# One core, a fused attention and feed-forward kernel: the first tiles' statistics taken in twos, the first product in halves, and other work and loads in another order at the head

## The reference

```python
xn = (x - mean(x)) / sqrt(var(x) + 1e-5)
q, k, v = xn @ Wq + bq, xn @ Wk + bk, xn @ Wv + bv      # 32, 8, 8 heads of 16
scores = einsum('bsdh,bseh->bsde', q, repeat(k, 4)) / 4
s = einsum('bsde,bseh->bsdh', softmax(scores), repeat(v, 4)).reshape(1, 2048, 512)
nx = xn * rsqrt(mean(xn ** 2) + 1e-5) * ln_w
ffn = (silu(nx @ gate_w.T) * (nx @ up_w.T)) @ down_w.T   # inner width 1792
out = x + s * silu(ffn)
```

## Time and profile before

| | before |
|---|---|
| median of 3 runs | 474.47 us (474.45 to 474.83) |
| profiled execution | 474.35 us |
| its span, first to last instruction | 472.6 us |
| PE busy | 466.3 us, 99% of the span |
| DVE, ACT, POOL busy | 412.7, 244.2 and 123.1 us |
| DMA | 105.70 MB, 224 GB/s in the mean |

### The profile page before, as it was taken

One profiled execution on the slowest core, in us unless ns is written; L12 is line 12 of the kernel. 1 busy time (PEld: TensorE's weight loads), 2 busy tenths in 40 slices (PEclk: granted clock), 3 DMA queues, 4 the chain that ended last, 5 costly groups with the idle time before them and its releaser, 6 DMA issues.

```text
span 472.6 us, 6217 instructions
## 1 busy us (share of the span) xinstructions
PE 466.3 (99%) x2122; PEld 391.0 (83%) x2122; DVE 412.7 (87%) x561; ACT 244.2 (52%) x417; POOL 123.1 (26%) x106
## 2 busy tenths in 40 slices
PE   7999999999999999999999999999999999999997
PEld 7898888888888888888888888888888888888886
DVE  6889778987898898889989898999998888888994
ACT  4785656658588888654122545225225335358102
POOL 5740312126222122233443101000011111126920
PEclk9999999999999999999999999999999999999999
DMA  8605996579779996573474649546556655514772
GB/s 269 252 2 225 345 380 262 234 259 273 205 248 301 298 360 255 188 268 133 135 235 162 218 187 371 202 184 223 222 201 223 223 200 200 201 44 135 276 259 89
DMA packets 44623, 105.70 MB, mean 224 GB/s; under 512 B 20272, under 2 KB 21808, under 8 KB 41264
## 3 DMA queue, kind: packets, MB, share of 16 engines
q1 hardware_dynamic: 44592, 105.31, 63.3%
HBM read 69.90 MB, written 35.40 MB: 223 GB/s over the span
## 4 chain that ended last, share of the span: by engine, by line
PE 95%; DVE 2%; DMA 1%; ACT 1%; SPq 0%; POOL 0%; issue 0%
PE gu_ps L553 18%; PE gu_ps L555 18%; PE gu_ps L556 18%; PE y_ps L687 8%; PE y_ps L688 8%; PE y_ps L689 8%; PE gu_ps L688 3%; PE gu_ps L687 3%; PE gu_ps L689 3%; PE gu_ps L718 2%; PE gu_ps L715 2%; PE gu_ps L714 2%; DMA xz<-x 1%; DVE w_ops L1166 1%; PE y_ps L727 0%; DVE stats L1075 0%
## 5 line engine op out<-in xcount | busy, mean ns | idle before, releaser
L553 PE MATMUL gu_ps<-z_hi,w_ops 128*128 128x512 f32 x378 | 147.2, 390 | 0.1
L556 PE MATMUL gu_ps<-z_hi,w_ops 128*128 128x512 f32 x378 | 147.1, 389 | 0.0
L555 PE MATMUL gu_ps<-z_lo,w_ops 128*128 128x512 f32 x378 | 147.1, 389 | 0.0
L498 POOL TENSOR_TENSOR h_lo<-h,h_hi 128x512 fp32r<-128x512 f32 x28 | 37.4, 1335 | 226.8 <-ACT h_hi L916 226.6
L553 PEld LDWEIGHTS gu_ps<-z_hi,w_ops 128*128 128x128 f32 x378 | 71.0, 188 | 15.5 <-issue 0.4
L556 PEld LDWEIGHTS gu_ps<-z_hi,w_ops 128*128 128x128 f32 x378 | 70.9, 188 | 14.8
L555 PEld LDWEIGHTS gu_ps<-z_lo,w_ops 128*128 128x128 f32 x378 | 70.9, 188 | 14.5
L687 PE MATMUL y_ps<-wd_ops,h_hi 128*128 128x512 f32 x168 | 65.6, 390 | 0.0
L689 PE MATMUL y_ps<-wd_ops,h_lo 128*128 128x512 f32 x168 | 65.5, 390 | 0.0
L688 PE MATMUL y_ps<-wd_ops,h_hi 128*128 128x512 f32 x168 | 65.5, 390 | 0.0
L916 ACT ACTIVATE h_hi<-h 128x512 fp32r<-128x512 f32 x28 | 17.6, 630 | 58.9 <-DVE h L1208 58.9
(11 more groups left out here) (139 smaller groups left out, 753.0 us busy)
## 6 DMA issues: line engine op xcount, KB each, us to landing
w_kept<-w_ops SPq DMA_DIRECT2D x13, 1792.0 KB, 6.2
w_ops<-w_kept SPq DMA_DIRECT2D x13, 1792.0 KB, 7.6
wd_ops<-wd_kept SPq DMA_DIRECT2D x35, 512.0 KB, 4.0
raw<-gate_up SPq DMA_DIRECT2D x30, 256.0 KB, 3.9
wd_kept<-wd_ops SPq DMA_DIRECT2D x14, 512.0 KB, 7.8
xz<-x SPq DMA_DIRECT2D x16, 256.0 KB, 5.3
raw<-down SPq DMA_DIRECT2D x14, 256.0 KB, 8.5
w_ops<-wd_kept SPq DMA_DIRECT2D x7, 512.0 KB, 7.5
```

The source lines that it names most:

```text
L498: pool.tensor_tensor(lo, src, hi.bitcast(F32), ALU.subtract).then_inc(h_lo_done, 1)
L553: pe.matmul(acc, w_h, z_hi[:, zi, c, :], start=start and c == 0, stop=False, skip_group_check=True)
L555: pe.matmul(acc, w_h, z_lo[:, zi, c, :], start=False, stop=False, skip_group_check=True)
L556: end = pe.matmul(acc, w_l, z_hi[:, zi, c, :], start=False, stop=c == 1, skip_group_check=True)
```

## The change

All of it is at the head, in the first 23 us or so.

- **DVE**: statistics of tiles 0 and 1, then `bn_aggr` for each and one instruction for both variances; the same for tiles 2 and 3; then the four normalisations in a row. `x_variance(0)` comes behind `first_lo(0)`.
- **POOL**: one root for two tiles, twice; then the queries' sums; then the root and shift of tile 4; only then `rms_of(0, ...)`, which stood ahead of the sums; then the bias sums and tiles 5 to 7 as before.
- **PE**: `first_gate0` and `first_up0` become `first_products`. Gate's high by high product is made in halves of 256 columns, each behind its two tiles; gate's product with the low activations likewise, and up's high by high product stands between its halves. `qkv_product(0)` waits for the split weights in two steps, not at once.
- **ACT**: issues the load of `lnw` itself, first of all; `first_hi(1)` stands ahead of `z_raw` of tiles 0 and 1.
- **SP**: no `lnw`; up is loaded ahead of the query weights; x tiles 5 and 6 ahead of the biases.

```diff
             load_x(0, range(0, J))
-            sp.dma_start(lnw_sb[:], lnw).then_inc(lnw_in, 16)
             load_gate(0)
+            load_up(0)
             for a in (0, 2):
                 sp.dma_start(wq_raw[:, a:a + 2, :], wq.rearrange("(k p) n -> p k n", p=P)[:, a:a + 2, :])\
                   .then_inc(wq_in[a // 2], 16)
-            load_up(0)
             sp.dma_start(wqkv_raw[:, :, DG:2 * DG], wk.rearrange("(k p) n -> p k n", p=P)).then_inc(wkv_in, 16)
             sp.dma_start(wqkv_raw[:, :, 2 * DG:], wv.rearrange("(k p) n -> p k n", p=P)).then_inc(wkv_in, 16)
-            load_x(0, (J,))
+            load_x(0, range(J, JJ - 1))
             sp.dma_start(bq_raw, bq.partition_broadcast(P)).then_inc(bias_in, 16)
...
-            load_x(0, range(J + 1, JJ))
+            load_x(0, (JJ - 1,))
...
+            def scale_two(j):
+                pool.wait_ge(var_done, j + 2)
+                t = slice(j, j + 2)
+                pool.tensor_tensor(z_scale[:, t], z_var[:, t], minus_half[:, t], ALU.pow).then_inc(z_scale_done, 2)
+
             def scale_tile(j):
-                pool.wait_ge(var_done, j + 1 + (j >= J))
-                t = slice(j, j + 1)
+                pool.wait_ge(var_done, j + 2)
+                t, m = slice(j, j + 1), slice(j - J, j - J + 1)
...
-            for j in range(J):
-                scale_tile(j)
-            pool.wait_ge(var_done, J + 1)
-            rms_of(0, J, 1, 0)
+            scale_two(0)
+            scale_two(2)
             sum_queries(0)
             sum_queries(1)
             scale_tile(J)
+            pool.wait_ge(var_done, J + 1)
+            rms_of(0, J, 1, 0)
             pool.wait_ge(bias_in, 48)
...
+                pe.wait_ge(w_hi_a, 1)
+                for a, t in enumerate(halves):
+                    pe.wait_ge(z_hi_done, 2 * a + 2)
+                    for n, (wi, zi, c) in enumerate(gates):
+                        pe.matmul(gate[:, t], w_part(0, wi, c), z_hi[:, zi, c, t], start=a + n == 0, stop=False,
+                                  skip_group_check=True)
+                pe.wait_ge(w_lo_a, 1)
+                for wi, zi, c in gates:
+                    pe.matmul(gate, w_part(1, wi, c), z_hi[:, zi, c, :], start=False, stop=False, skip_group_check=True)
+                pe.wait_ge(z_lo_done, 2)
+                for wi, zi, c in gates:
+                    pe.matmul(gate[:, halves[0]], w_part(0, wi, c), z_lo[:, zi, c, halves[0]], start=False, stop=False,
+                              skip_group_check=True)
+                pe.wait_ge(w_hi_a, 2)
+                for n, (wi, zi, c) in enumerate(ups):
+                    pe.matmul(up, w_part(0, wi, c), z_hi[:, zi, c, :], start=n == 0, stop=False)
+                pe.wait_ge(z_lo_done, J)
...
-                pe.wait_ge(wqkv_hi_done, 2)
                 for k in range(K):
+                    if index == 0:
+                        pe.wait_ge(wqkv_hi_done, k // 2 + 1)
...
-                pe.wait_ge(wqkv_lo_done, 2)
                 for k in range(K):
+                    if index == 0:
+                        pe.wait_ge(wqkv_lo_done, k // 2 + 1)
...
+            act.dma_start(lnw_sb[:], lnw).then_inc(lnw_in, 16)
             load_silu()
...
+            first_hi(1)
             z_raw_tile(0)
             z_raw_tile(1)
-            first_hi(1)
...
+            for j in (0, 2):
+                stats_tile(j)
+                stats_tile(j + 1)
+                aggregate(j)
+                aggregate(j + 1)
+                two_variances(j)
             for j in range(J):
-                stats_tile(j)
-                if j:
-                    variance(j - 1)
-                if j > 1:
-                    normalise_tile(j - 2)
-            variance(J - 1)
-            normalise_tile(J - 2)
+                normalise_tile(j)
+            first_lo(0)
             x_variance(0)
-            normalise_tile(J - 1)
-            first_lo(0)
             for j in range(J):
                 z_lo_tile(j)
```

More of the change, by code:

```diff
@@ L575, in eight, with first_products, w_part @@
                 return end
-            def first_gate0():
-                acc = gu_ps[:, GATE_BANK, :]
-                chunks = [(wi, zi, c) for wi, zi in ((WA11, ZB11), (WA12, ZB21)) for c in range(2)]
-                pe.wait_ge(w_hi_a, 1)
-                pe.wait_ge(z_hi_done, J)
-                for n, (wi, zi, c) in enumerate(chunks):
-                    pe.matmul(acc, w_ops[:, 0, 0, wi, c * P:(c + 1) * P], z_hi[:, zi, c, :], start=n == 0, stop=False)
-                pe.wait_ge(w_lo_a, 1)
-                for wi, zi, c in chunks:
-                    pe.matmul(acc, w_ops[:, 0, 1, wi, c * P:(c + 1) * P], z_hi[:, zi, c, :], start=False, stop=False)
+            def first_products():
+                gate, up = gu_ps[:, GATE_BANK, :], gu_ps[:, UP_BANK, :]
+                gates = [(wi, zi, c) for wi, zi in ((WA11, ZB11), (WA12, ZB21)) for c in range(2)]
+                ups = [(wi, zi, c) for wi, zi in ((WA21, ZB11), (WA22, ZB21)) for c in range(2)]
+                halves = slice(0, TB // 2), slice(TB // 2, TB)
+                def w_part(s, wi, c):
+                    return w_ops[:, 0, s, wi, c * P:(c + 1) * P]
+                pe.wait_ge(w_hi_a, 1)
+                for a, t in enumerate(halves):
[3 more added lines that the diff above has]
+                                  skip_group_check=True)
+                pe.wait_ge(w_lo_a, 1)
+                for wi, zi, c in gates:
[7 more added lines that the diff above has]
+                    pe.matmul(up, w_part(0, wi, c), z_hi[:, zi, c, :], start=n == 0, stop=False)
@@ L587, in first_gate0 @@
                 pe.wait_ge(z_lo_done, J)
-                for n, (wi, zi, c) in enumerate(chunks):
-                    end = pe.matmul(acc, w_ops[:, 0, 0, wi, c * P:(c + 1) * P], z_lo[:, zi, c, :], start=False,
-                                    stop=n == 3)
+                for n, (wi, zi, c) in enumerate(gates):
+                    end = pe.matmul(gate[:, halves[1]], w_part(0, wi, c), z_lo[:, zi, c, halves[1]], start=False,
+                                    stop=n == 3, skip_group_check=True)
@@ L591, in first_gate0 @@
                 end.then_inc(m2_done, 1)
-            def first_up0():
-                acc = gu_ps[:, UP_BANK, :]
-                chunks = [(wi, zi, c) for wi, zi in ((WA21, ZB11), (WA22, ZB21)) for c in range(2)]
-                pe.wait_ge(w_hi_a, 2)
-                for n, (wi, zi, c) in enumerate(chunks):
-                    w_h = w_ops[:, 0, 0, wi, c * P:(c + 1) * P]
-                    pe.matmul(acc, w_h, z_hi[:, zi, c, :], start=n == 0, stop=False)
-                    pe.matmul(acc, w_h, z_lo[:, zi, c, :], start=False, stop=False)
+                for wi, zi, c in ups:
+                    pe.matmul(up, w_part(0, wi, c), z_lo[:, zi, c, :], start=False, stop=False)
@@ L601, in first_up0 @@
                 pe.wait_ge(w_lo_a, 2)
-                for n, (wi, zi, c) in enumerate(chunks):
-                    end = pe.matmul(acc, w_ops[:, 0, 1, wi, c * P:(c + 1) * P], z_hi[:, zi, c, :], start=False,
-                                    stop=n == 3)
+                for n, (wi, zi, c) in enumerate(ups):
+                    end = pe.matmul(up, w_part(1, wi, c), z_hi[:, zi, c, :], start=False, stop=n == 3)
                 end.then_inc(m4_done, 1)
@@ L1056, in _, with aggregate, two_variances, variance @@
         def _(dve):
-            def variance(j):
+            def aggregate(j):
                 dve.wait_ge(bn_done, j + 1)
                 dve.bn_aggr(mean_var[:, j, :], stats[:, j, :]).then_inc(stats_done, 1)
+            def two_variances(j):
+                dve.wait_ge(stats_done, j + 2)
+                dve.tensor_scalar(z_var[:, j:j + 2], mean_var[:, j:j + 2, 1], 1.0 + EPS, EPS * EPS,
+                                  ALU.mult, ALU.add).then_inc(var_done, 2)
+            def variance(j):
                 dve.wait_ge(stats_done, j + 1)
```

12 lines of the change are left out of this document (5 added, 7 removed).

## The result

| | before | after |
|---|---|---|
| median, taken in turns on one chip | 474.65 us (474.45 to 474.99, 4 runs) | 478.94 us (478.04 to 479.6, 4 runs) |
| profiled execution | 474.35 us | 479.6 us |
| its span | 472.6 us | 477.8 us |
| mean granted clock in it | 1.00 | 0.996 |

The ratio is 1.009, with an interval of 1.0072 to 1.0108: slower by 4.3 us, where 475.6 (+1.15) was forecast and 476.4 was the end of the range. The direction was right and the size was not.

A forecast was written before the change was run, and what follows sets the result against it. PE was taken to bound the kernel, its head paced by a tight line from POOL's tile 5 root to tile 2's product. -1.09 + 2.3 = +1.21, less 0.05 rounding, +1.15: 475.6 us, range 474.1 to 476.4.

The forecast's parts named there:

- -1.09 (sums sooner): POOL's queries' sums start at 10.35, not 11.44, so tile 4's statistics and shift come 1.09 us sooner.
- +2.3 (`rms_of` on the line): On POOL, `rms_of` now stands between tile 4's shift and the bias sums, delaying tile 5's root by 2.3 us.
- The clock: Rival D: PE's waits of 1.5 and 0.8 us drop it to 1.2 GHz, 2 us on top, 477.6; 4%.
- None of this reaches the tight line: Statistics in twos and `lnw` on ACT don't affect the line from POOL's tile 5 root to PE's tile 2 product.
- the bound of 0.48: Delay of an x tile from loading `lnw` on ACT's queue: between 0 and one issue step, 0.48 us.
- The product in halves at nothing: On PE, tile 0's first query product comes about 1.4 us sooner, then PE waits for tile 4: no gain.
- the shape of the wait: PE waits 1.5 us ahead of tile 5's transposes, then 0.8 us between those and tile 6's.
- The prediction's marks: Signs: POOL's 128x4 roots at 17.4 to 19.5, PE waiting over 2 us for `xz`, tile 2's product about 24.
- B: Rival: POOL's pair of `rms_of` roots is covered, POOL free some 0.9 us sooner: 474.4 to 475.3; 23%.
- C: Rival: transfers limit the head and all moves sooner; PE keeps 1.4 us from the first product: 473.1; 11%.
- B's own condition: `lo_qkv` on DVE comes later than POOL's tile 4 root, which alone takes 0.56 us, not 1.26.

The follow-up runs named there:

- a_lnw_sp: After, with the load of `lnw` back on SP behind x tiles 0 to 3: 476.9 us, ratio 1.0037 against before.
- a_sum_wait: After, with POOL's queries' sums waiting until DVE has made the low parts of gate's weights: 476.98 us, ratio 1.0042 against before.
- b_rms_late: Before, with one edit: `rms_of` moved behind tile 4's root and shift on POOL: 478.62 us, ratio 1.0075 against before.
- b_halves: Before, with only the PE and ACT part: first products in halves, finer waits, `first_hi(1)` ahead of `z_raw`: 474.83 us, ratio 0.9996.
- a_up_back: After, with up loaded behind the query weights again, `lnw` still on ACT: 477.66 us, ratio 1.0066 against before.
- a_lnw_fill: After, with `lnw` loaded by SP and 12 and 6 added transposes in PE's waits: 478.09 us, ratio 1.0068 against before.

## Why the prediction was wrong, by its own steps

- **The step that failed: "-1.09 (sums sooner)".** It took the sums' earlier start as a gain in full, and tile 4's statistics came 1.75 us later and not 1.09 sooner, an error of 2.84. Of this 2.42 is DVE held by the sums: 1.65 in `first_lo(0)` and 0.77 in the last normalisation. The other 0.42 is what the term was over-sized by without a collision, as far as one profile tells: in a_lnw_sp, where the sums missed `first_lo(0)`, tile 4's statistics came 0.66 sooner. The forecast of 475.6 with that error put right is 478.4, and after's two runs at full clock took 478.45 and 478.04. The prediction let the sums start at 10.35 and read `first_lo(0)` with the 1.05 that it took beside other work. It asked what the sums would be *rid* of (the overlap with `first_lo(1)`) and never what stood on DVE at the place that they move *to*. Its own rows had both: the query weights lay there from 9.6 on in before, and `first_lo(0)` ran from 9.56 to 10.61. With up ahead it let the weights land at 10.3; in after they let the sums start at 9.83, and these met the last normalisation and three of the four of `first_lo(0)`. The landing alone doesn't explain the error: from 10.35 on the sums would have met `first_lo(0)` too, which could start at 10.3 at the soonest (an estimate: 11.07 less 0.77).
- **The rule that was applied at one place only.** The prediction cited the Trainium skill, "SBUF — State Buffer", section "Who interferes with whom", and said that it speaks against a pure gain, but used it only for `first_lo(1)` and put no price on the place that the sums move to. By it a DVE instruction with two SBUF inputs and a GpSimd instruction that reads SBUF exclude each other. a_sum_wait and b_rms_late agree: four instructions of 0.34 us take 1.13 in all ahead of the sums and 2.77 to 3.66 beside them. Before doesn't, in one place: POOL's roots of 128x4 read SBUF too, and beside them the same four took no longer. There the measurement decides.
- **"+2.3 (`rms_of` on the line)" held**: 2.21 in the trace, 2.1 at tile 5's root when undone. So did its place, and the distance from there to PE.
- **"The clock", 4%, was too little.** The mechanism was named with its place; what was missing was how likely it is. It came in two of four runs and costs 1.56 us in the profiled one (said: 2). PE's waits were 1.34 and 0.56 us, less than the 1.5 and 0.8 that the rival assumed.
- **"None of this reaches the tight line", for the statistics in twos and `lnw`, held only in before's order.** Tile 3's statistics began 0.61 later in after's profile (7.14 against 6.53), more than the bound of 0.48, and the third and fourth normalisation wait for one root. Neither is dear by itself; together they moved `first_lo(0)` 0.8 us later, and the held normalisation as much again, to 11.07, under the sums. The root of 128x2 took 0.71 and 0.87 where 0.7 was taken.
- **The product in halves at nothing held** (b_halves, in before's order), and so did the shape of the wait. The prediction's marks were met late: roots of `rms_of` at 20.2 (said 17.4), tile 2's product at 26.8 (said 24).
- **Rivals B and C** needed an earlier head and fell with it. B's own condition didn't come either: tile 4's root lay beside `lo_qkv` again and took 1.26 us.

**What stays open.** Why tile 3 lands at 6.6 to 7.2 in the five profiles of variants of after that have `lnw` on ACT, and at 5.7 to 6.6 in the other nine, is not settled: `lnw` on ACT alone didn't do it, and b_rms_late, with before's loads unchanged, had 6.6 too. Nor is it settled what decides in which execution the clock falls: a_up_back had the same two waits of PE (1.9 us in all) and fell in none of four runs.

## What to carry to other kernels

Before an instruction is moved to an earlier place on POOL, write down what DVE runs in the stretch that it moves into, not only in the one that it leaves; two neighbours in a written order can be there as a shield without saying so. If two instructions hold each other, fix their order with a wait, where it costs less than the collision: it buys a small spread too. And take a link out of the chain from the last engine backwards: a step that is hidden in a wait of 5 us on one side of a dependency costs its full length on the other.

## What the runs showed of the hardware

- A fp32 `scalar_tensor_tensor` on DVE, 128x128, takes 0.34 us alone and up to 1.17 beside POOL's sums; a `tensor_scalar` of 128x512 takes 0.54 alone and 1.32 beside the first of them (after). The held instruction lasts about as long as the POOL instruction beside it (0.64 to 0.72 for those of 128x256, 1.04 to 1.21 for those of 128x512). POOL's roots of 128x4 in before, beside the same group, held nothing.
- Two waits of PE, 1.34 and 0.56 us with 0.6 us of transposes between them, were followed in some executions by 3.4 us (after, a_lnw_sp) of matmuls at 1.2 GHz, starting within a microsecond of PE's being at work again. The Trainium skill, "TensorE: Matmul & The Clock Gate", section "HAM oscillation — how this bites in real kernels", tells of such falls behind idle stretches between bursts; the trace agrees in kind, though not in each execution.
- The same loads in the same order can land 1 us apart in two executions: the first part of the query weights let the sums start at 9.77 in a_lnw_fill and at 10.77 in a_lnw_sp, whose loads are the same. An order between two engines that rests on such a landing is only as firm as their waits.
